# Weight loads of a three-part transformer kernel moved within the queue that issues them

## Chip, cores and metric

The kernel runs on one core of a Trainium2 chip, in one launch. The metric is device time: 3499.77 us, the median of three runs (3498.44 to 3503.96).

## The reference

The input is 4 sequences of 512 tokens with 128 features, in float32. Four stages follow one another, each added to its input and each applied to the layer-normalised activations: a chunked linear attention, a transformer of 6 layers, a retention layer with decay, and the same 6-layer transformer again, with the same weights. The transformers take nearly all the time. One layer of them is, in the reference's terms:

```python
def shift_tokens(t):            # second half of the features comes from the token before
    a, s = jnp.split(t, 2, -1)
    s = jnp.pad(s, ((0, 0), (1, 0), (0, 0)))[:, :-1]
    return jnp.concatenate([a, s], -1)
def attn_layer(x, Wqkv, qs, ksc, Wo):     # 16 heads of 64
    q, k, v = jnp.split(x @ Wqkv, 3, -1)
    ...
    q = l2norm(q) * qs
    k = l2norm(k) * ksc
    # rotary turn with a scale that grows by position, in q, and its inverse in k
    out = local_attention(q, k, v)        # windows of 32 queries on 64 keys, softmax
    return out @ Wo
def ffn_layer(x, g, bln, W1, b1, W2, b2): # 128 -> 2 x 341 -> 128
    xn = (x - mu) / jnp.sqrt(var + 1e-05) * g + bln
    a, gate = jnp.split(xn @ W1 + b1, 2, -1)
    return a * jax.nn.gelu(gate, approximate=False) @ W2 + b2
for i in range(DEPTH):
    x = attn_layer(shift_tokens(x), ...) + x
    x = ffn_layer(shift_tokens(x), ...) + x
```

## The kernel before

Activations stay on chip, transposed (features on partitions), in `xT` and `zT`. `stage_a`, `stage_ffn(0)`, `stage_b`, `stage_ffn(1)` and `finish` run in that order. The change is in `stage_ffn`, which is used twice; we call the two uses phase 0 and phase 1.

**Steps.** `stage_ffn` goes through 24 pairs of layer and sequence (6 layers, 4 sequences each) and makes one step of each pair. A step is a software pipeline of two halves: `cur` is the attention of the sequence at hand, `prev` is the rest of the sequence before it: its last values, output projection, and the whole second part of the layer (gates, hidden values, second product). So 25 steps run, 0 to 24; step 0 has no `prev`, step 24 no `cur`. The first step of a new layer is step 4, 8, ...; its `prev` half still belongs to the old layer. The output weights `wout` and the second-stage weights `w1`, `w2`, `pf` of a new layer are therefore needed one step later than its projection weights.

**Quads.** The 16 heads are worked in 4 quads of 4 heads. For each quad PE projects queries and keys (L626 to L628; the weights are split in two parts, `wh` and `wl`, and the product made in three matmuls), ACT squares the result (L809) and scales it into `ab` (L810), POOL adds the squares (L923), PE sums them over the head (`norms`, L645), ACT makes the inverse norms (L821, L823), DVE and POOL turn and scale (L964 to L978, L927 to L932). Then SP copies keys and queries to the layout that the score matmuls want, PE makes the scores (`scores`, L663), DVE subtracts the maximum (L984, L987), ACT takes exponentials (L827), DVE normalises and transposes (L993 to L1002), SP copies the transposed probabilities to `tb`, and PE multiplies them with the values (`values`, L684). ACT's `evacuate(g)` for quad g waits for the key and query copies of quad g - 2 (L805, L806), since they read the half of `ab` that it overwrites. PE's `values(g)` waits for the copies of the probabilities (`t_dma`, L675).

**The order on each engine is written out by hand.** Every engine has a function `step(s, prev, cur)` that lists its work in order, and they meet in semaphores that count up over the whole run; `now.count(signal, at)` gives the value to wait for. An engine takes its instructions in order, so whatever stands behind a waiting one waits as well.

**SP is the queue of the transfers.** All transfers within the loop are issued by SP. Its helpers in `step` are: `keys(g)`, 8 transfers of 64 KB (L516), after a wait for the turned keys; `queries(g)`, 4 of 128 KB (L526); `weights(g)`, 8 of the probabilities (L534 to L539), after a wait for the transpose `p_tr`; `next_tokens()`, 2 (L546, L547). The name weights(g) is for attention weights, that is probabilities, not for parameters; an index of -1 means quad 3 of the sequence before. The order within a step is keys(0), queries(0), next_tokens, weights(-1), keys(1), queries(1), weights(0), keys(2), queries(2), weights(1), keys(3), queries(3), weights(2).

**Parameters.** `load_qkv(rows, quads)` issues three transfers for a quad (384 KB, 384 KB and 2 KB; L479, L480), `load_out` one of 512 KB (L483), `load_ff` four (341, 128, 42.5 and 4.5 KB; L486 to L489). In the last step of a layer (3, 7, ..., 19) the projection weights of the next layer are loaded: quad 0 ahead of keys(2), quad 1 behind queries(2), quads 2 and 3 at the end, behind weights(2). In the first step of the new layer (4, 8, ..., 20) `wout` is loaded behind queries(2) and `load_ff` stands at the end, behind weights(2) and a wait for `x2`, the last addition of the sequence before, which no longer needs the old weights. PE waits for `w_ff` ahead of the gate matmuls (L779).

**SP's loops.** Step 0 stands alone. Then comes an outer loop over the layer changes (L589) whose body has an inner loop over two ordinary steps (L584), the step that loads the next layer, and the first step of the new layer. Behind the loop an inner loop over three ordinary steps and step 24 follow. The body holds the code of three steps for four that run. The other engines have one plain loop over steps 1 to 23.

`SP_USES` lists the multipliers and offsets of the counts that SP waits for, so that they can be computed once a step.

Of the kernel before, what the change touches and what calls it, by code (L numbers as in the profile page):

```python
# [3 lines left out]
def build_hybrid(nc, x_in, tabs, wa, wb, wf, out):  # L4
# [13 lines left out]
    B, N = 4, 512  # L18
    TOK = B * N
    DEPTH, HEADS, DH, WIN = 6, 16, 64, 32  # L20
# [10 lines left out]
    with ctx:  # L31
# [331 lines left out]
        STEPS = DEPTH * B  # L363
# [30 lines left out]
        x2 = Signal("x2", 1, 1, 4)  # L394
# [3 lines left out]
        w_out, w_ff = Signal("w_out", 16), Signal("w_ff", 64)  # L398
        GRANTED = [xs_done, x_hi, x_lo, n_ready, rope_q, rope_k, k_dma, q_dma, s_ready, s_sub, p_tr, t_dma, *o_ready, *o_read, x2, val_done]

        SP_USES = [(1, -1), (1, 0), (1, 1), (1, 3), *((4, c) for c in range(-2, 2)), (8, -4), (8, 0)]
        PE_USES = [(1, -1), (1, 0), (1, 2), (2, -2), (3, -5), (3, -4), (3, -3), (3, 0), *((4, c) for c in range(-4, 1)),
                    *((8, c) for c in (-12, -8, -7, -6, -5, -4, -3, -2, -1, 0)), *((16, c) for c in range(-15, 1)),
                    *((256, c) for c in range(-128, 65, 64)), *((512, c) for c in range(-640, 129, 128))]
# [7 lines left out]
        def stage_ffn(phase):  # L412
            scope = ExitStack()
            with scope:
# [33 lines left out]
                L0, FIRST = phase * DEPTH, phase * STEPS  # L448
# [17 lines left out]
                def _(sp):  # L466
# [15 lines left out]
                    def load_out(at):  # L482
                        sp.dma_start(wout[:, :, :], wf["wout"][bass.ds(at, 1)].rearrange("l (k p) n -> p (l k) n", p=128)).then_inc(w_out.sem, 16)  # L483

                    def load_ff(at):
                        sp.dma_start(w1[:, :], wf["w1"][bass.ds(at, 1)].rearrange("l c n -> (l c) n")).then_inc(w_ff.sem, 16)  # L486
                        sp.dma_start(w2[:, 0:2, :], wf["w2"][bass.ds(at, 1), 0:256].rearrange("l (k p) n -> p (l k) n", p=128)).then_inc(w_ff.sem, 16)
                        sp.dma_start(w2[0:FFC[2], 2, :], wf["w2"][bass.ds(at, 1), 256:FF].rearrange("l p n -> (l p) n")).then_inc(w_ff.sem, 16)
                        sp.dma_start(pf[:, :], wf["pf"][bass.ds(at, 1)].rearrange("l c n -> (l c) n")).then_inc(w_ff.sem, 16)  # L489
# [7 lines left out]
                        sp.dma_start(dst, src).then_inc(consts, 16)  # L497
                    load_qkv(rows_of_layer(0), range(1, QUADS))
                    load_out(0)
                    load_ff(0)  # L500

                    def step(s, prev, cur, new_layer=None, next_layer=None):
                        now = Steps(sp, s + 1, SP_USES)

                        if next_layer is not None:
# [22 lines left out]
                        def weights(g):  # L528

                            sp.wait_ge(o_ready[1].sem, now.count(o_ready[1], g - 1))  # L530
                            sp.wait_ge(p_tr.sem, now.count(p_tr, g))
                            for r in range(4):
                                rows = slice(32 * r, 32 * r + 32)
                                sp.dma_start(tb[rows, r], ptb[rows, 1]).then_inc(t_dma.sem, 16)  # L534

                                if r:
                                    sp.dma_start(tb[32 * r - 32:32 * r, r], ptb[rows, 0]).then_inc(t_dma.sem, 16)
                                else:
                                    sp.dma_start(tb[96:128, 4, 0:12], ptb[rows, 0, 4:16]).then_inc(t_dma.sem, 16)  # L539
# [12 lines left out]
                            next_tokens()  # L552
                        if prev:
                            weights(-1)
                        if cur:
                            keys(1)
                            queries(1)
                            weights(0)
                            if next_layer is not None:


                                sp.wait_ge(v_ready.sem, now.count(v_ready, TILES - 1))
                                load_qkv(layer_rows, range(1))
                            keys(2)
                            queries(2)
                            if next_layer is not None:
                                load_qkv(layer_rows, range(1, 2))
                            if new_layer is not None:
                                sp.wait_ge(wo_ready.sem, now.count(wo_ready, -1))
                                load_out(new_layer)  # L570
                            weights(1)
                            keys(3)
                            queries(3)
                            weights(2)
                            if next_layer is not None:

                                sp.wait_ge(v_ready.sem, now.count(v_ready, 2 * TILES - 1))
                                load_qkv(layer_rows, range(2, QUADS))
                            if new_layer is not None:
                                sp.wait_ge(x2.sem, now.count(x2, -1))  # L580
                                load_ff(new_layer)

                    def later_sequences(first, end):
                        with sp.Fori(1, end) as b:  # L584
                            step(first + b, True, True)

                    sp.wait_ge(zeroed, 2)
                    step(FIRST, False, True)
                    with sp.Fori(1, DEPTH) as at:  # L589
                        later_sequences(FIRST - B + at * B, B - 1)  # L590
                        step(FIRST - 1 + at * B, True, True, next_layer=at)
                        step(FIRST + at * B, True, True, new_layer=at)
                    later_sequences(FIRST + STEPS - B, B)
                    step(FIRST + STEPS, True, False)

                @block.tensor
# [738 lines left out]
```

## Time and profile before

| | |
|---|---|
| median of three runs | 3499.77 us |
| lowest, highest | 3498.44, 3503.96 us |
| the profiled execution | 3499.11 us |
| span of its trace | 3497.3 us |
| PE busy | 3165.8 us, 91% |
| DVE busy | 2895.0 us, 83% |
| ACT busy | 2273.7 us, 65% |
| POOL busy | 1808.8 us, 52% |
| mean granted TensorE clock | 0.951 |
| issues of f_kb, f_tb | 1536 of 64 KB, 1344 of 64 KB; 2.0 us to landing |
| issues of f_qb | 768 of 128 KB; 2.4 us to landing |
| issues of f_wh, f_wl | 48 each of 384 KB; 3.3 and 3.5 us to landing |

The busy times are sums over the whole span. PE is the busiest, but its share says nothing of when it stands still; that is read from the rows of single instructions. SP has no busy time in this table, since issuing a transfer isn't counted; its issues stand in the timeline as rows of SPq, with the time that each took to issue. "To landing" is the time from the issue to the arrival of the last byte. In the part of phase 0 between 541 and 1566 us lie steps 5 to 20, in the part of phase 1 between 2200 and 3260 us most of steps 4 to 20.

### The profile page before, as it was taken

What the parts mean: (1) busy time and instruction counts of PE and PEld (TensorE: products, weight loads), DVE (VectorE), ACT (ScalarE), POOL (GpSimd) and SP (SyncE); (2) the same over time, 40 slices, a digit from 0 to 9 for tenths busy, and PEclk for the clock granted to TensorE, in tenths of its full rate; (3) what the DMA queues carried; (4) which work ended last, traced back from release to release, by engine and by line L of the source; (5) the groups of instructions that cost most, each with busy time, mean ns of one, the idle gap of its engine ahead of it and who ended that gap; (6) DMA issues with size and microseconds to landing.
All of it is one profiled execution on the core that took longest, in us unless ns stands there. A gap on an engine that the chain in (4) does not pass through costs nothing. (4 is left out here: it accounts for less than half of the span.)

```text
span 3497.3 us, 71552 instructions
## 1 busy us (share of the span) xinstructions
PE 3165.8 (91%) x25368; PEld 1997.4 (57%) x25560; DVE 2895.0 (83%) x2723; ACT 2273.7 (65%) x3693; POOL 1808.8 (52%) x823
## 2 busy tenths in 40 slices
PE   5769999999999999999956899999999999999996
PEld 3536655655656666666533566666666566566563
DVE  4559988988988988988924899898898898898994
ACT  1147776766766776777712677677777777777773
POOL 5535555555555555555500555555565555555551
PEclk8789999999999999999977999999999999999998
DMA  5444454454454554554411445445445445445442
GB/s 183 160 116 101 111 135 107 116 127 109 115 130 107 122 124 104 122 127 108 99 34 66 101 104 140 114 97 144 109 103 141 110 105 140 105 111 137 111 111 60
DMA packets 273778, 399.12 MB, mean 114 GB/s; under 512 B 75836, under 2 KB 104248, under 8 KB 273720
## 3 DMA queue, kind: packets, MB, share of 16 engines
q1 hardware_dynamic: 273720, 398.48, 46.4%
q8 instruction: 20, 0.33, 0.0%
q14 instruction: 38, 0.31, 0.0%
HBM read 66.34 MB, written 19.92 MB: 25 GB/s over the span
## 5 line engine op out<-in xcount | busy, mean ns | idle before, releaser
L927 POOL TENSOR_TENSOR f_w<-f_w,f_ab 128x1024 f32<-128x1024 f32 x192 | 554.9, 2890 | 568.2 <-DVE f_w L964 568.2
L923 POOL TENSOR_TENSOR f_u<-f_u 128x512 f32<-128x512 f32 x384 | 582.0, 1530 | 464.0 <-ACT f_u L809 464.0
L932 POOL TENSOR_TENSOR f_ab<-f_w,f_rn 128x1024 f32<-128x1024 f32 x192 | 588.3, 3064 | 321.8 <-DVE f_rn L974 310.7
L809 ACT ACTIVATE f_u<-ps 128x512 f32<-128x512 f32 x768 | 466.6, 608 | 162.9 <-PE ps L628 84.9
L810 ACT ACTIVATE f_ab<-ps,f_pa 128x512 f32<-128x512 f32 x768 | 540.8, 704 | 1.2
L964 DVE TENSOR_TENSOR f_w<-f_ab,f_tan 128x1024 f32<-128x1024 f32 x384 | 498.9, 1340 | 4.6 <-POOL f_ab L932 4.6
L626 PE MATMUL ps<-f_xh,f_wh 128*128 128x512 f32 x768 | 384.2, 500 | 118.3 <-ACT f_ab L810 100.6
L684 PE MATMUL ps<-f_tb,f_v 128*64 128x160 f32 (+1 forms) x6144 | 446.9, 299 | 18.4 <-DMA f_tb<-f_pt 17.1
L684 PEld LDWEIGHTS ps<-f_tb,f_v 128*64 128x64 f32 x6144 | 400.2, 139 | 107.7 <-issue 105.0
L663 PEld LDWEIGHTS ps<-f_kb,f_qb 128*32 128x32 f32 x12288 | 351.2, 117 | 161.4 <-issue 128.3
L821 ACT ACTIVATE ps<-ps 128x512 f32<-128x512 f32 x384 | 204.6, 574 | 359.2 <-PE ps L645 359.2
L663 PE MATMUL ps<-f_kb,f_qb 128*32 128x128 f32 x12288 | 409.5, 290 | 24.5 <-DMA f_qb<-f_ab 24.5
L645 PE MATMUL ps<-f_u,f_ones 128*128 128x512 f32 x768 | 371.0, 605 | 9.1 <-DVE f_ones L1074 6.5
L699 PE MATMUL ps<-f_ot,f_wout 128*128 128x512 f32 x768 | 366.5, 600 | 1.7 <-DVE zT L1062 1.7
L984 DVE TENSOR_REDUCE f_mx<-ps 128x16 f32<-128x1024 f32 x192 | 233.3, 1215 | 140.1 <-PE ps L663 139.2
L827 ACT ACTIVATE f_p<-f_p 128x1024 f32<-128x1024 f32 x192 | 203.2, 1058 | 198.6 <-DVE f_p L987 198.6
L993 DVE TENSOR_REDUCE f_rs<-f_p 128x16 f32<-128x1024 f32 x192 | 233.4, 1216 | 116.5 <-ACT f_p L827 116.5
L978 DVE TENSOR_TENSOR f_ab<-f_w,f_rn 128x1024 f32<-128x1024 f32 x192 | 310.6, 1618 | 6.6
L628 PE MATMUL ps<-f_xh,f_wl 128*128 128x512 f32 x768 | 308.8, 402 | 0.0
L627 PE MATMUL ps<-f_xl,f_wh 128*128 128x512 f32 x768 | 307.7, 401 | 0.0
L999 DVE TENSOR_TENSOR f_p<-f_p,f_rs 128x1024 f32<-128x1024 f32 x192 | 280.6, 1462 | 1.8
L626 PEld LDWEIGHTS ps<-f_xh,f_wh 128*128 128x128 f32 x768 | 147.6, 192 | 233.4 <-ACT f_ab L810 138.4
(169 smaller groups left out, 5034.2 us busy)
## 6 DMA issues: line engine op xcount, KB each, us to landing
f_kb<-f_ab SPq DMA_DIRECT2D x1536, 64.0 KB, 2.0
f_qb<-f_ab SPq DMA_DIRECT2D x768, 128.0 KB, 2.4
f_tb<-f_pt SPq DMA_DIRECT2D x1344, 64.0 KB, 2.0
f_wh<-split_w SPq DMA_DIRECT2D x48, 384.0 KB, 3.3
f_wl<-split_w SPq DMA_DIRECT2D x48, 384.0 KB, 3.5
a_w_raw<-wqkv SPq DMA_DIRECT2D x24, 384.0 KB, 4.0
split_w<-a_w_hi SPq DMA_DIRECT2D x24, 384.0 KB, 2.3
split_w<-a_w_lo SPq DMA_DIRECT2D x24, 384.0 KB, 2.8
```

Source lines behind the costliest of these rows:

```text
L626: nc.tensor.matmul(bank("qk", g, i), wh[:, g, i, :], xh[:, :], start=True, stop=False)
L645: last = nc.tensor.matmul(ps[:, NO[i], :], ones[:, :], u[:, 2 * i + 1, :], start=True, stop=True)
L663: last = nc.tensor.matmul(ps[rows, SS[tile // 2], c0:c0 + 128], qb[:, pair, w0:w0 + WIN], kb[:, pair, :, w0:w0 + 2 * WIN], start=False, st ...
L684: last = nc.tensor.matmul(ps[rows, NO[pair], 128 * tile:128 * tile + WIN * windows], v[:, tile, d0:d0 + 64], tb[:, 0:windows, tile * HQ + ...
L699: last = nc.tensor.matmul(f, wout[:, 2 * g + i, :], ot[:, 2 * g + i, :], start=g + i == 0, stop=g + i == QUADS)
L809: nc.scalar.activation(u[:, i, :], bank("qk", g, i), ACT.Square).then_inc(sq_done.sem, 1)
L810: nc.scalar.activation(ab[:, g % 2, i, :], bank("qk", g, i), ACT.Identity, scale=pa[:, g, i:i + 1]).then_inc(qk_read.sem, 1)
L923: nc.gpsimd.tensor_tensor(u[:, 2 * i + 1, :], u[:, 2 * i, :], u[:, 2 * i + 1, :], ALU.add).then_inc(sq_sum[i].sem, 1)
L927: nc.gpsimd.tensor_tensor(w[:, 0:2, :], w[:, 0:2, :], ab[:, k % 2, 0:2, :], ALU.add).then_inc(q_sum.sem, 1)
L932: nc.gpsimd.tensor_tensor(ab[:, k % 2, 0:2, :], w[:, 0:2, :], rn[:, 0:1, :].broadcast_to([128, 2, N]), ALU.mult).then_inc(rope_q.sem, 1)
L964: nc.vector.tensor_tensor(w[:, a:4:2, :], ab[:, k % 2, 1 - a:4:2, :], tan2[:, a:a + 1, :].broadcast_to([128, 2, N]), ALU.mult).then_inc(tu ...
L978: nc.vector.tensor_tensor(ab[:, k % 2, 2:4, :], w[:, 2:4, :], rn[:, 1:2, :].broadcast_to([128, 2, N]), ALU.mult).then_inc(rope_k.sem, 1)
```

## The change

`load_ff` is taken out of the start of a phase and out of the end of a new layer's first step. In its place it stands in the step after that (steps 1, 5, 9, ..., 21), behind weights(-1) and ahead of keys(1), behind a wait for `x2` of two sequences back. The loads of quads 2 and 3 in the last step of a layer, with their wait for the last value projection, move from behind weights(2) to ahead of it. The inner loops are written out as steps, so that the one with `hidden_layer` can differ: the body of the outer loop then holds the code of four steps. `SP_USES` gets the offset that the new wait needs.

```diff
-        SP_USES = [(1, -1), (1, 0), (1, 1), (1, 3), *((4, c) for c in range(-2, 2)), (8, -4), (8, 0)]
+        SP_USES = [*((1, c) for c in range(-1, 3)), *((4, c) for c in range(-2, 2)), (8, -4), (8, 0)]
...
                     load_out(0)
-                    load_ff(0)
-
-                    def step(s, prev, cur, new_layer=None, next_layer=None):
+
+                    def step(s, prev, cur, hidden_layer=None, next_layer=None, new_layer=None):
...
                         if prev:
                             weights(-1)
+                        if hidden_layer is not None:
+
+                            sp.wait_ge(x2.sem, now.count(x2, -2))
+                            load_ff(hidden_layer)
                         if cur:
                             keys(1)
...
                             keys(3)
                             queries(3)
-                            weights(2)
                             if next_layer is not None:
 
                                 sp.wait_ge(v_ready.sem, now.count(v_ready, 2 * TILES - 1))
                                 load_qkv(layer_rows, range(2, QUADS))
-                            if new_layer is not None:
-                                sp.wait_ge(x2.sem, now.count(x2, -1))
-                                load_ff(new_layer)
-
-                    def later_sequences(first, end):
-                        with sp.Fori(1, end) as b:
-                            step(first + b, True, True)
+                            weights(2)
 
                     sp.wait_ge(zeroed, 2)
                     step(FIRST, False, True)
                     with sp.Fori(1, DEPTH) as at:
-                        later_sequences(FIRST - B + at * B, B - 1)
+                        step(FIRST - 3 + at * B, True, True, hidden_layer=at - 1)
+                        step(FIRST - 2 + at * B, True, True)
                         step(FIRST - 1 + at * B, True, True, next_layer=at)
                         step(FIRST + at * B, True, True, new_layer=at)
-                    later_sequences(FIRST + STEPS - B, B)
+                    step(FIRST + STEPS - 3, True, True, hidden_layer=DEPTH - 1)
+                    with sp.Fori(1, 3) as b:
+                        step(FIRST + STEPS - 3 + b, True, True)
                     step(FIRST + STEPS, True, False)
```

## Rows read from the trace of the kernel before

**Rows 1.** The page, part 1: busy us (share) x instructions of each engine.

```profile
PE 3165.8 (91%) x25368; PEld 1997.4 (57%) x25560; DVE 2895.0 (83%) x2723; ACT 2273.7 (65%) x3693; POOL 1808.8 (52%) x823
```

**Rows 2.** Timeline of DVE: start, us, line; steps 1, 3, 4, 5, 23; 1, 23.

```profile
326.94 0.68 DVE L1055 TENSOR_TENSOR f_xl<-f_xs,f_xh 128x512 fp32r<-128x512 f32 x1
...
450.20 0.68 DVE L1055 TENSOR_TENSOR f_xl<-f_xs,f_xh 128x512 fp32r<-128x512 f32 x1
...
515.80 0.68 DVE L1055 TENSOR_TENSOR f_xl<-f_xs,f_xh 128x512 fp32r<-128x512 f32 x1
...
584.06 0.68 DVE L1055 TENSOR_TENSOR f_xl<-f_xs,f_xh 128x512 fp32r<-128x512 f32 x1
...
1735.24 0.68 DVE L1055 TENSOR_TENSOR f_xl<-f_xs,f_xh 128x512 fp32r<-128x512 f32 x1
...
2031.40 0.68 DVE L1055 TENSOR_TENSOR f_xl<-f_xs,f_xh 128x512 fp32r<-128x512 f32 x1
...
3428.28 0.68 DVE L1055 TENSOR_TENSOR f_xl<-f_xs,f_xh 128x512 fp32r<-128x512 f32 x1
```

**Rows 3.** Timeline of ACT, first square of quad 2; steps 3, 4, 5, 21; [idle before].

```profile
417.95 0.59 ACT L809 ACTIVATE f_u<-ps 128x512 f32<-128x512 f32 x1
...
482.14 0.60 ACT L809 ACTIVATE f_u<-ps 128x512 f32<-128x512 f32 x1 [2.48 <-DMA f_qb<-f_ab]
...
550.00 0.60 ACT L809 ACTIVATE f_u<-ps 128x512 f32<-128x512 f32 x1 [4.76 <-DMA f_qb<-f_ab]
...
1578.28 0.60 ACT L809 ACTIVATE f_u<-ps 128x512 f32<-128x512 f32 x1 [1.80 <-DMA f_qb<-f_ab]
```

**Rows 4.** Timeline of SP's issues around the starts of steps 3, 4, 5; phase 1's 5.

```profile
408.17 4.96 SPq L516 DMA_DIRECT2D f_kb<-f_ab  x8
...
464.47 0.54 SPq L534 DMA_DIRECT2D f_tb<-f_pt  x1
...
472.78 4.95 SPq L516 DMA_DIRECT2D f_kb<-f_ab  x8
...
534.48 0.59 SPq L537 DMA_DIRECT2D f_tb<-f_pt  x1
...
536.94 0.36 SPq L489 DMA_DIRECT2D f_pf<-pf  x1
540.65 4.95 SPq L516 DMA_DIRECT2D f_kb<-f_ab  x8
...
2242.68 0.35 SPq L489 DMA_DIRECT2D f_pf<-pf  x1
2243.90 4.95 SPq L516 DMA_DIRECT2D f_kb<-f_ab  x8
```

**Rows 5.** Source line L589; DMA queues from 541 to 1566 us: packets, MB, share.

```profile
L589 SPq COMPARE_BRANCH  x10: 40/45/45, 537.4 to 3261.9; - x10
...
q14 instruction: 18, 0.15, 0.0%
```

**Rows 6.** PE in timeline and windows (PE busy, clock, DMA share, GB/s).

```profile
410.29 2.29 PE L684 MATMUL ps<-f_tb,f_v 128*64 128x160 f32 x32
...
484.00:487.00 3.00, 3.00 (x50) 0.50 0.46 109
...
1579.51 0.79 PE L626 MATMUL ps<-f_xh,f_wh 128*128 128x512 f32 x1 [2.67 <-ACT f_ab L810]
...
2000.47 0.50 PE L626 MATMUL ps<-f_xh,f_wh 128*128 128x512 f32 x1 [1.56 <-ACT f_ab L810]
```

**Rows 7.** Page, part 6, keys; then L516 from 477 to 477.7 us.

```profile
f_kb<-f_ab SPq DMA_DIRECT2D x1536, 64.0 KB, 2.0
...
DMA to landing us min/median/max: 2.6/2.8/3.0
```

**Rows 8.** Timeline of step 2: SP's keys(1) and PE's scores(1).

```profile
361.27 4.99 SPq L516 DMA_DIRECT2D f_kb<-f_ab  x8
...
372.07 1.95 PE L663 MATMUL ps<-f_kb,f_qb 128*32 128x128 f32 x64
```

## Prediction

> Steps are numbered within a phase as in the code: step 0 to step 24, each with the second half of the sequence before it. Steps 3, 7, 11, 15, 19 load the next layer's projection weights ("next steps"), steps 4, 8, 12, 16, 20 are the first of a new layer ("new steps"), steps 5, 9, 13, 17, 21 follow them ("hidden steps"). Quads are 0 to 3.
>
> **What bounds the kernel now.** I read the page's table of busy time first: PE 91%, no other engine above 83% [rows 1]. The chain of waits that ended last gives nothing here: it breaks off at once at the last addition on DVE. So I took one DVE instruction that runs once a step (L1055) from the timeline and took its distances [rows 2]. Steps 1 to 3 are 123.26 us apart over two intervals, 61.63 each. The interval that ends in new step 4 is 65.60, the one that ends in hidden step 5 is 68.26. From step 1 to step 23 there are 22 intervals, 1408.30 us in phase 0 and 1396.88 in phase 1; at 61.6 each they would be 1355.2. So 53.1 + 41.7 = 94.8 us is all that layer changes cost, 10 new and 10 hidden steps, and no edit of the weight loads can win more.
>
> Where it is lost shows in ACT's rows at the first square of quad 2 (L809) [rows 3]. In step 3 it starts at 417.95 with no idle time. In step 4 ACT idles 2.48 us before it, in step 5 4.76, in step 21 1.80, each time for the query transfers of quad 0 (`queries(0)`). PE then stands still, since its banks aren't read out, and comes back at a granted clock of 0.50, that is 1.2 instead of 2.4 GHz [rows 6]: that is the remainder of the excess (65.60 - 61.6 - 2.48 = 1.5 us in step 4). So a boundary costs its ACT stall plus some 1.5 us of low clock; step 21, with 1.80, some 3.3.
>
> And the queries are late because SP, which issues every transfer at about 0.62 us each, is late with `keys(0)` [rows 4]. In step 3 keys(0) starts at 408.17; a step later it would be due at 469.8 and starts at 472.78, because the loads of quads 2 and 3 stand between weights(2) and it: weights(2) starts at 464.47, eight issues take it to 469.45, the loads take 3.3 us. Before step 5 weights(2) ends at 534.48 + 0.59 = 535.07, `load_ff` at 537.30, and then SP issues nothing until 540.65: 5.58 us from weights(2) to keys(0). In phase 1 the same place shows 2243.03 to 2243.90, a gap of 0.87 rather than 3.35.
>
> That gap is code. Here the outer loop of SP branches back (L589, ten times); between 541 and 1566 us, phase 0, the DMA view has 18 packets of instructions, and none between 2200 and 3260, phase 1 [rows 5]. The bodies are the same; so phase 0's just doesn't stay in the engine's instruction store, and phase 1's just does.
>
> **The change, part by part.**
>
> *(a) Loads of quads 2 and 3 ahead of weights(2), 10 places.* SP's time is conserved: from the start of keys(3) to keys(0) it runs without a pause (queries(3) ends at 464.37, weights(2) starts at 464.47), the v_ready wait has long been met, so weights(2) starts 3.1 us later and keys(0) of the new step still starts at 472.8. The stall of quad 2 isn't removed. What is new: the last of the eight transfers is issued at 472.0 instead of 468.86. Behind such loads a 64 KB transfer at the same distance took 2.8 us to land instead of the 2.0 of an undisturbed one [rows 7]: 474.8 to 475.0. PE's `values(-2)` (L684), which needs them, starts at 410.29 in step 3, so is due at 471.9 in step 4 [rows 6]. PE waits 2.9 us there. Behind it stand the rest of project_v(0), norms(1), and by them ACT's inverse_norms(1) and quad 2: ACT is ready for quad 2 at 479.66 + 2.9 = 482.6, the queries are there at 482.14. The two delays lie beside each other, and +0.5 us is left. The clock: PE idle for 2.67 us came back with its matmul at 0.79 us, PE idle for 1.56 us at 0.50 [rows 6], so 2.9 us costs the same 1.5 us as now, only earlier; the second pause is then under 1 us. Value: 10 x 0.5 = +5. Ends: -1.0 a place if the clock isn't lowered (0.5 - 1.5), +2.0 if it is lowered twice (0.5 + 1.5); I take the middle because 2.9 is nearer to the row of 2.67 than to that of 1.56.
>
> *(b) load_ff out of the turn from the new to the hidden step.* Phase 0, four turns over the outer branch (steps 5, 9, 13, 17): the 2.2 us of load_ff go, the 3.35 of the branch stay, keys(0) and queries(0) come 2.2 us earlier, the ACT stall falls from 4.76 to 2.6. That is still a pause like step 4's, so the low clock stays: -2.2 x 4 = -8.8. Ends: 0 and, if stall and clock both went, -6.6 a place.
>
> Phase 1, four turns: the body now writes out four steps instead of looping over one of three (each about 82 transfers and some 15 other instructions), so it is over a quarter longer. What overflowed in phase 0 at the shorter length should now overflow in both. The gap grows from 0.87 to 3.35 while 2.2 us go: +0.3 x 4 = +1.2. Ends: +0.3 a place, and -3.7 if the code still stays.
>
> The Trainium skill ("Runtime: NRT & Kernel Launch", Instruction fetch mechanics) says that an engine holds two blocks of 256 instructions and that a taken branch out of these stops for a fetch. The trace agrees with the stop and shows its price, 3.35 us less some 0.5 of register work. By that rule a body of about 436 instructions would stay if it started in the first 76 of a block, three times in ten. It is the rule that would bring rival 2 below.
>
> Last turn of each phase (into step 21): no branch back, neither before nor after. load_ff goes, keys(0) follows weights(2) as from step 2 to 3, and stall and clock go: -3.3 x 2.
>
> *(c) load_ff between weights(-1) and keys(1) of steps 1, 5, ..., 21.* It adds four issues and a wait for x2 of two steps back, done long before (its writer L1062 runs half a step earlier): 2.2 us. Queued behind it are keys(1), queries(1), weights(0). In an undisturbed step keys(1) starts at 361.27 and PE's scores(1) (L663) at 372.07 [rows 8]. Eight issues of keys and four of queries put the last at 368.2; with the 2.4 us that the page's table of transfers gives for f_qb it lands at 370.6. So the slack is 1.5 us, 0.7 us come through to PE, and half of that is lost again in ACT's own queue, which is the longer one there: +0.4 in steps 1 and 21 (4 in all: +1.6). In steps 5 to 17 keys(1) waits for scores(0) anyway (the low clock draws these scores out, and SP is there first), so it is hidden. Ends: 0 and +0.7. w1 and w2 are needed some 25 us later by PE's gate matmuls; hidden. The loads taken out of the start of each phase stood ahead of a wait of 5 us and more for the first keys: nothing. The inner loop's branch (0.7 us) lay in slack: nothing.
>
> **Sum.** +5.0 - 8.8 + 1.2 - 6.6 + 1.6 = -7.6 us. The profiled execution took 3499.11 (span 3497.3 and 1.8 around it) and the median is 3499.77; from the latter the forecast is 3492 us. The measurement tells about 0.2%, 7 us, from nothing, so this lies on the edge of what can be told.
>
> **Rivals.**
> 1. PE's pause at values(-2) doesn't lower the clock (two pauses of 2.9 and under 1 us instead of one of 3.35). For it: 1.56 us didn't. Against: 2.67 did. It saves 1.5 in each of 10 places: 3492 - 15 = 3477.
> 2. The longer body stays in the store in phase 1. For it: the body fits there now, and the page's rule. Against: the same body doesn't fit in phase 0. Then each of four turns is 0.9 us from weights(2) to keys(0) instead of 3.1, stall and clock go, -3.7 instead of +0.3: 3492 - 16 = 3476.
> 3. Slower: weights(2) behind 1.5 MB of loads. The eight transfers of probabilities queue behind the loads, values(-2) waits over 4 us, and PE comes back slow, so that ACT's quad 2 is later than the queries by more than the parts (b) give: these are worth 12.6 us, so the point is 1.3 us a place over ten places. For it: transfers right behind the loads are visibly slower [rows 7] and the slack at values(-2) is only about 1 us (last issue some 0.95 ahead of 408.17, landing at 409.2, use at 410.29). Against: five microseconds of issuing lie between the last load and the last of them. At +2.5 a place: 3499.8 + 25 - 12.6 = 3512; at +2.0, 3507.
> 4. The change moves things only: (a) costs 1 us a place, or fetches fall on other places, and all cancels: 3497 to 3503.
>
> **Chances.** Forecast 50% (3485 to 3498, 27 of the 50 below 3492.8, the rest within 0.2%), rival 1 14%, rival 2 10%, rival 3 15%, rival 4 11%. Faster by over 0.2%: 27 + 14 + 10 = 51%; within: 23 + 11 = 34%; slower: 15%. The range takes in both faster rivals but their tails and rival 3 up to +2.0: 3474 to 3507.
>
> **What would show it.** In the new steps keys(0) still about 3 us late and ACT's stall before quad 2 gone or small, with a PE wait before L684 for the probabilities of 2 to 3 us in its place; if that wait isn't there, (a) is wrong. In hidden steps of both phases a gap of some 3.3 us on SP before keys(0), with instruction packets in phase 1 too, and an ACT stall of 2.6; no gap in phase 1 is rival 2. Into step 21 an interval of 62. L1055's distances give the sum directly: per layer 66.1 and 66.1 in phase 0, 66.1 and 65.7 in phase 1.

## The result: 0.9926 of the time before

The changed kernel took 3475.39 us (median of 4 runs, 3471.86 to 3479.21), the kernel before beside it 3499.82 (3498.44 to 3503.96). The ratio is 0.9926, with a 95% interval of 0.9914 to 0.9938: 24.4 us faster, where 7.6 were forecast. The time lies at the fast edge of the range, where rivals 1 and 2 stood.

The profiled execution took 3471.86 us (span 3470.1, mean granted clock 0.958). First the page's busy times, beside [rows 1]: PE is busy 20 us less with the same number of matmuls. The work is the same; some of it ran at the higher clock.

```profile
PE 3145.8 (91%) x25368; PEld 1982.1 (57%) x25560; DVE 2906.5 (84%) x2723; ACT 2275.1 (66%) x3693; POOL 1816.8 (52%) x823
```

DVE's instruction that runs once a step (L1054 now), timeline; steps 1, 3, 4, 5, 23 of phase 0, then 1 and 23 of phase 1, as in [rows 2]:

```profile
332.94 0.68 DVE L1054 TENSOR_TENSOR f_xl<-f_xs,f_xh 128x512 fp32r<-128x512 f32 x1
...
456.20 0.68 DVE L1054 TENSOR_TENSOR f_xl<-f_xs,f_xh 128x512 fp32r<-128x512 f32 x1
...
520.57 0.68 DVE L1054 TENSOR_TENSOR f_xl<-f_xs,f_xh 128x512 fp32r<-128x512 f32 x1
...
586.06 0.68 DVE L1054 TENSOR_TENSOR f_xl<-f_xs,f_xh 128x512 fp32r<-128x512 f32 x1
...
1721.44 0.68 DVE L1054 TENSOR_TENSOR f_xl<-f_xs,f_xh 128x512 fp32r<-128x512 f32 x1
...
2016.64 0.68 DVE L1054 TENSOR_TENSOR f_xl<-f_xs,f_xh 128x512 fp32r<-128x512 f32 x1
...
3403.84 0.68 DVE L1054 TENSOR_TENSOR f_xl<-f_xs,f_xh 128x512 fp32r<-128x512 f32 x1
```

New step 4 is 64.37 us (65.60 before), hidden step 5 65.49 (68.26 before). The 22 intervals of a phase make 1388.50 and 1387.20 us; over the 1355.2 of undisturbed steps that is 33.3 + 32.0 = 65.3, where it was 94.8.

ACT's first square of quad 2 in steps 3, 4, 5 and 21, as in [rows 3]; in brackets the idle time before it:

```profile
423.96 0.60 ACT L808 ACTIVATE f_u<-ps 128x512 f32<-128x512 f32 x1
...
488.41 0.60 ACT L808 ACTIVATE f_u<-ps 128x512 f32<-128x512 f32 x1 [0.33 <-DMA f_qb<-f_ab]
...
552.41 0.60 ACT L808 ACTIVATE f_u<-ps 128x512 f32<-128x512 f32 x1 [2.38 <-DMA f_qb<-f_ab]
...
1565.97 0.60 ACT L808 ACTIVATE f_u<-ps 128x512 f32<-128x512 f32 x1
```

The stall of step 4 is 0.33 us (2.48), that of step 5 2.38 (4.76), that of step 21 gone (1.80). Then SP's issues, as in [rows 4]; the last two lines are phase 1's hidden step 5:

```profile
414.06 4.94 SPq L515 DMA_DIRECT2D f_kb<-f_ab  x8
...
473.86 0.56 SPq L533 DMA_DIRECT2D f_tb<-f_pt  x1
...
479.05 4.95 SPq L515 DMA_DIRECT2D f_kb<-f_ab  x8
...
539.47 0.58 SPq L536 DMA_DIRECT2D f_tb<-f_pt  x1
543.05 4.95 SPq L515 DMA_DIRECT2D f_kb<-f_ab  x8
...
2224.84 0.59 SPq L536 DMA_DIRECT2D f_tb<-f_pt  x1
2228.48 4.95 SPq L515 DMA_DIRECT2D f_kb<-f_ab  x8
```

In step 4 keys(0) starts 3.39 us later than a step of 61.6 after step 3's: SP is still as late as before (3.01 then), even 0.4 us later. In hidden steps the gap from weights(2) to keys(0) is 3.00 us in phase 0 (5.58 before) and 3.05 in phase 1 (3.09 before, most of it load_ff then). The DMA queues from 541 to 1566 us (phase 0) and from 2200 to 3260 (phase 1), packets, MB, share, beside [rows 5]:

```profile
q14 instruction: 24, 0.20, 0.1%
```

```profile
q14 instruction: 21, 0.17, 0.0%
```

Phase 1 had no packet of instructions before. It has 21 now.

**The budget.** ACT's squares of quad 3 give each step's length. Summed over 61.6, in us, for two traces of each kernel (the second pair is from the runs after_again and before_again below):

```
                        forecast   before        after         measured change
10 new steps            +5.0       44.8, 44.4    35.4, 41.4     -6.2
hidden 5..17, phase 0   -8.8       27.1, 27.0    15.4, 14.2    -12.3
hidden 5..17, phase 1   +1.2       16.3, 16.2    14.4, 14.3     -1.9
two steps 21            -6.6 +0.8   6.4,  6.7     0.1,  0.1     -6.4
two steps 1             +0.8        1.4,  1.7     3.9,  3.4     +2.1
sum                     -7.6                                   -24.7
```

So the forecast missed in the first three lines: by 11.2 us in the new steps, where even the sign was wrong, and by 3.5 and 3.1 in the turns. The steps of the table make 24.7 us, but the traces' spans differ by 21.0 in the mean (3497.3 and 3495.3 before, 3470.1 and 3480.6 after). Nearly all of the rest is the time before phase 0's first L1055, at 205.60 and 210.51 us before and at 211.12 and 212.18 after; over all traces of this study it lies between 205.6 and 213.6, and nothing here explains it.

### The profile page after: what moved, and what is told of

Read it like the earlier page. It is cut to its first block and busy times, and to the rows that moved or that the text cites. A ratio compares the mean times of both kernels' runs of the same rounds, so it can differ in the third digit from the quotient of the medians.

```text
span 3470.1 us, 71421 instructions
## 1 busy us (share of the span) xinstructions
PE 3145.8 (91%) x25368; PEld 1982.1 (57%) x25560; DVE 2906.5 (84%) x2723; ACT 2275.1 (66%) x3693; POOL 1816.8 (52%) x823
## 5 line engine op out<-in xcount | busy, mean ns | idle before, releaser
L922 POOL TENSOR_TENSOR f_u<-f_u 128x512 f32<-128x512 f32 x384 | 589.4, 1549 | 452.6 <-ACT f_u L808 451.9
L683 PE MATMUL ps<-f_tb,f_v 128*64 128x160 f32 (+1 forms) x6144 | 452.6, 301 | 44.9 <-DMA f_tb<-f_pt 43.6
L683 PEld LDWEIGHTS ps<-f_tb,f_v 128*64 128x64 f32 x6144 | 404.4, 140 | 135.6 <-issue 99.9
L662 PEld LDWEIGHTS ps<-f_kb,f_qb 128*32 128x32 f32 x12288 | 338.0, 113 | 158.7 <-issue 119.0
L662 PE MATMUL ps<-f_kb,f_qb 128*32 128x128 f32 x12288 | 392.9, 282 | 28.0 <-DMA f_qb<-f_ab 27.9
L714 PE MATMUL ps<-f_fq,f_w 128*128 128x512 f32 (+1 forms) x576 | 271.2, 609 | 7.6 <-issue 5.9
```

The lines of the kernel that those rows point to most:

```text
L662: last = nc.tensor.matmul(ps[rows, SS[tile // 2], c0:c0 + 128], qb[:, pair, w0:w0 + WIN], kb[:, pair, :, w0:w0 + 2 * WIN], start=False, st ...
L683: last = nc.tensor.matmul(ps[rows, NO[pair], 128 * tile:128 * tile + WIN * windows], v[:, tile, d0:d0 + 64], tb[:, 0:windows, tile * HQ + ...
L922: nc.gpsimd.tensor_tensor(u[:, 2 * i + 1, :], u[:, 2 * i, :], u[:, 2 * i + 1, :], ALU.add).then_inc(sq_sum[i].sem, 1)
```

## The experiments

The theory that they test: PE's pause ahead of values(-2), which the moved loads bring, is about 2.8 us long, and at this length the lower clock follows only in some places, while the forecast took it for all. Rivals are that the new body, or part (b), brought the gain, and that the loads themselves (1.5 MB in flight) and not the pause decide about the clock. Ratios are to the kernel before on the same chip, with 95% intervals; "new" and "hidden" are the sums over ten such steps, as in the budget (before: 44.8 and 49.8). Where a step is said to have the lower clock, the trace grants 0.50 for a stretch behind its pause.

**Part (a) alone.** The kernel before with the block moved up:

```diff
+    if next_layer is not None:
+        sp.wait_ge(v_ready.sem, now.count(v_ready, 2 * TILES - 1))
+        load_qkv(layer_rows, range(2, QUADS))
     weights(2)
-    if next_layer is not None:
-        sp.wait_ge(...); load_qkv(...)
```

> The kernel before with part (a) alone: the loads of quads 2 and 3 ahead of weights(2). Theory: keys(0) of the new step stays as late as it was, PE now pauses 2.4 to 3.1 us before values(-2) instead of 3.4 us before quad 2, and in most of the 10 places that pause doesn't lower the clock. New steps then cost 2.8 us over an ordinary one where the clock stays and 4.7 where it falls, against 4.0 to 5.3 before; about -10 us in all, 3490 us. Rival: (a) gives nothing by itself, the gain is all of load_ff's move: 3500 us, new steps at 4.0 to 5.3 over. My own prediction had 3505.

3494.71 against 3500.20 us, 0.9982 (0.9972 to 0.9992). New 37.2, hidden 46.0. The new steps gain 7.6 where the forecast had them lose 5; in four of the ten places they are 2.5 to 2.9 us over, in the others 3.8 to 5.0. In phase 1 three hidden steps (2.26, 2.28 and 1.79 over) lack the lower clock too. The two steps 1 were 5.7 over (before 1.4), without part (c); with these 4.3 us the whole came to 3495 instead of the 3490 expected.

**Parts (b) and (c) alone.** The changed kernel with weights(2) back ahead of the loads:

```diff
+    weights(2)
     if next_layer is not None:
         sp.wait_ge(...); load_qkv(layer_rows, range(2, QUADS))
-    weights(2)
```

> The changed kernel with the loads of quads 2 and 3 put back behind weights(2): load_ff's move and the written-out body alone. Theory: hidden steps 3.5 to 3.9 us over an ordinary one in both phases, step 21 none, new steps as before (4.0 to 5.3), the first steps of a phase some 1.2 us slower each: 3499.8 - 20 + 2.4 = 3482 to 3485 us. Rival, that (a) gives nothing: 3475 us.

3489.04 us, 0.9966 (0.9954 to 0.9979). Hidden 29.3, which is after's 29.8, and new 48.8. So (a) gains in the new steps (7.6) and (b) in the hidden ones (20.5), as the budget has it for both together. By the medians the parts make 5.5 + 11.2 = 16.7 of 24.4 us. What lacks is in the steps 1 (7.3 over here, 1.4 before) and in this kernel's new steps, 4.0 above before: ACT's stalls in front of quad 2 are 2.3 us longer there in sum (28.2 against 25.8), and in six of the ten places, not four, the lower clock lasted longer and cost 2.3 us and more (below). Why the stalls and the steps 1 are longer is open.

**The longer body alone.** The kernel before with its inner loop written out and the loads of w1 and w2 at their old places:

```diff
     with sp.Fori(1, DEPTH) as at:
-        later_sequences(FIRST - B + at * B, B - 1)
+        step(FIRST - 3 + at * B, True, True)
+        step(FIRST - 2 + at * B, True, True)
```

> The kernel before with the body of the outer loop written out as four steps, nothing moved. If SP's pause at the branch back is code that no longer stays in its store: instruction packets in phase 1 too, the gap before keys(0) of steps 5, 9, 13, 17 in phase 1 grows from 0.87 to 3.3 us, with load_ff still ahead of it, so these four steps go from 3.7 to some 6.5 us over an ordinary one: +11 us, 3511 us. Rival: the longer body stays, or the gap has another cause (registers, the x2 wait): 3500 us and no packets.

3518.41 us, 1.0055 (1.0038 to 1.0071), slower. Hidden steps of phase 1: 30.6 instead of 19.5, +11.1. The timeline of SP in phase 1's step 5 shows the last issue before the branch and keys(0):

```profile
2251.44 0.36 SPq L489 DMA_DIRECT2D f_pf<-pf  x1
2255.05 4.97 SPq L516 DMA_DIRECT2D f_kb<-f_ab  x8
```

3.25 us without an issue, where [rows 4] has 0.87; and from 2200 to 3260 us 24 packets of instructions:

```profile
q14 instruction: 24, 0.20, 0.1%
```

So it is the written-out body that brings the stop at the branch into phase 1, by itself, and the rest of part (b) that pays for it. The gain isn't the body's. Phase 0's hidden steps lost 3.7 us as well, 1.7 of it in step 21; that part, and the 7 us by which the time lies over the expected 3511, were not followed up.

**The same loads, one turn earlier.** The changed kernel with the block between weights(1) and keys(3), where SP has slack:

```diff
     weights(1)
+    if next_layer is not None:
+        sp.wait_ge(...); load_qkv(layer_rows, range(2, QUADS))
     keys(3)
     queries(3)
-    if next_layer is not None:
-        sp.wait_ge(...); load_qkv(layer_rows, range(2, QUADS))
     weights(2)
```

> The changed kernel with the loads of quads 2 and 3 between weights(1) and keys(3), where SP idles 3.5 us for the turned keys. Theory: the loads (3.3 us of issuing) fit there, keys(0) of the new step is on time, neither PE nor ACT pauses, new steps cost 0 to 0.5 us over an ordinary one instead of 2.8 to 4.7: -33 us, 3442 us. Rival 1: keys(3) or its landing gets late by the 1.5 MB in front of it, and 1 us a place comes back: 3452. Rival 2: what a new step costs isn't SP's lateness but its new weights: 3475, as it is.

3441.28 us, 0.9839 (0.9821 to 0.9857). The DVE instruction of steps 3, 4 and 5:

```profile
454.67 0.68 DVE L1054 TENSOR_TENSOR f_xl<-f_xs,f_xh 128x512 fp32r<-128x512 f32 x1
...
516.27 0.68 DVE L1054 TENSOR_TENSOR f_xl<-f_xs,f_xh 128x512 fp32r<-128x512 f32 x1
...
580.63 0.68 DVE L1054 TENSOR_TENSOR f_xl<-f_xs,f_xh 128x512 fp32r<-128x512 f32 x1
```

New step 4 takes 61.60 us. New 0.0, hidden 28.9: the whole of a new step's excess comes of the 3.2 us of issuing between two transfers that are waited for.

The hidden steps, where only the branch is left, show the clock once more. PE's first matmul behind its pause, in step 5 of phase 0 and of phase 1:

```profile
549.14 0.50 PE L625 MATMUL ps<-f_xh,f_wh 128*128 128x512 f32 x1 [3.09 <-ACT f_ab L809]
...
2211.16 0.80 PE L625 MATMUL ps<-f_xh,f_wh 128*128 128x512 f32 x1 [3.13 <-ACT f_ab L809]
```

Behind the first the clock stayed up and the step is 2.8 us over, behind the second it fell and the step is 4.8 over. All four turns of phase 0 kept the clock, with pauses of 3.07 to 3.25 us, and all four of phase 1 lost it, with 3.09 to 3.14.

**The loads split.** The changed kernel with quad 2's loads ahead of weights(2) and quad 3's behind:

```diff
-    load_qkv(layer_rows, range(2, QUADS))
+    load_qkv(layer_rows, range(2, 3))
     weights(2)
+    if next_layer is not None:
+        load_qkv(layer_rows, range(3, QUADS))
```

> The changed kernel with the load of quad 2 ahead of weights(2) and that of quad 3 behind it. SP's time to keys(0) is the same. Theory: what a new step costs is SP's lateness of 2.5 to 2.8 us; the low clock comes on top only where one single pause of PE is long. Here the pause is cut in two, some 1.2 us at values(-2) and some 2 us ahead of quad 2, so the clock stays in all 10 places: new steps at 2.5 to 2.8 over an ordinary one, 26 us instead of 35 in sum, 3466 us. Rival: the sum of the pauses decides, or chance: new steps still at 4 or more in several places, 3475 us.

3470.25 against 3502.68 us, 0.9918 (0.9901 to 0.9934). New 36.7: five phase 0 steps with 5.61, 5.62, 4.15, 4.33 and 2.87, and phase 1's five with 2.78 to 2.84. PE's pause is now ahead of quad 2; its timeline after such a pause, step 4 of phase 0 and of phase 1:

```profile
485.81 0.79 PE L627 MATMUL ps<-f_xh,f_wh 128*128 128x512 f32 x1 [2.80 <-ACT f_ab L811]
...
2172.63 0.50 PE L627 MATMUL ps<-f_xh,f_wh 128*128 128x512 f32 x1 [2.78 <-ACT f_ab L811]
```

Two pauses of one length, 2.80 and 2.78 us, and the first matmul behind them takes 0.79 us once and 0.50 the other time. Four of phase 0's five places had the lower clock, none of phase 1's. I had expected the new steps at 26 and two short pauses; the one at values(-2) was 0.8 to 0.9 us and left the other at 2.8. Without the lower clock a place costs 2.8 us, near the 2.5 to 2.8 expected; that the clock would stay up was wrong.

**No loops on SP.** The changed kernel with its steps written out one by one, so that nothing branches and all addresses and counts are constants:

```diff
-    with sp.Fori(1, DEPTH) as at:
-        step(FIRST - 3 + at * B, True, True, hidden_layer=at - 1)
-        ...
+    for n in range(1, STEPS):
+        step(FIRST + n, True, True, hidden_layer=..., next_layer=..., new_layer=...)
```

> The changed kernel with SP's 25 steps written out without a loop, nothing moved. Theory: the hidden steps' cost (3.5 to 3.9 us each in 8 places) is the fetch of code behind SP's branch back; straight code is fetched ahead. No gap before keys(0) of steps 5, 9, 13, 17, no ACT stall there: -28 us, 3447 us; new steps as they are. Rival: the fetches of straight code, one each 128 instructions, stop SP as well, spread over all steps: ordinary steps over 61.6 us and 3475 us or more.

3454.90 against 3502.68 us, 0.9862 (0.9845 to 0.9878). Steps 3, 4 and 5 on DVE:

```profile
457.04 0.68 DVE L1049 TENSOR_TENSOR f_xl<-f_xs,f_xh 128x512 fp32r<-128x512 f32 x1
...
523.45 0.68 DVE L1049 TENSOR_TENSOR f_xl<-f_xs,f_xh 128x512 fp32r<-128x512 f32 x1
...
585.06 0.68 DVE L1049 TENSOR_TENSOR f_xl<-f_xs,f_xh 128x512 fp32r<-128x512 f32 x1
```

Hidden step 5 takes 61.61 us, and all ten together are 0.2 over: with load_ff moved, what is left of a hidden step is the branch with its register work. Straight code fetched as well (12 packets of instructions from 541 to 1566 us) and stopped nothing. The new steps cost 51.3 here, more than before the change: the eighth transfer of probabilities landed 2.9 to 3.7 us after its issue (2.0 to 2.8 in the changed kernel), the pauses were 2.86 to 3.69 us, and nine of ten had the lower clock. So the kernel came to 3455 instead of the 3447 expected.

**Both.** The kernel without loops and with the loads one turn earlier, that is, on top of the edit of flat:

```diff
     weights(1)
+    if next_layer is not None:
+        load_qkv(layer_rows, range(2, QUADS))
     keys(3)
     queries(3)
```

> Both: no loop on SP, and the loads of quads 2 and 3 between weights(1) and keys(3). Theory: every step of both phases at 61.6 us but the first ones: 3441 - 28 = 3413 us. Rival: straight code stops SP for fetches: 3441 or more.

3407.73 us, 0.9733 (0.9717 to 0.9749), 5 us under the expected 3413. And the same with layer 0's w1 and w2 loaded at the start of each phase again, so that step 1 has no such loads:

```diff
     load_out(0)
+    load_ff(0)
...
-    hidden_layer=n // B if n % B == 1 else None
+    hidden_layer=n // B if n % B == 1 and n > 1 else None
```

> flat_early with the first layer's load_ff back at the start of each phase, so that step 1 has none ahead of keys(1). Theory: load_ff cost the two steps 1 1.2 us each in the changed kernel where its addresses came from registers; with constants, as here and in step 21, it costs about nothing: 0 to -2.4 us against flat_early, 3411 to 3413 us. Rival: at the start it delays the first keys: +3 us a phase, 3419.

3404.36 us, 0.9723 (0.9707 to 0.9740), the fastest version of this study, 71 us below the changed kernel. Steps 1 and 23 of each phase on DVE:

```profile
329.85 0.68 DVE L1050 TENSOR_TENSOR f_xl<-f_xs,f_xh 128x512 fp32r<-128x512 f32 x1
...
1685.39 0.68 DVE L1050 TENSOR_TENSOR f_xl<-f_xs,f_xh 128x512 fp32r<-128x512 f32 x1
...
1978.48 0.68 DVE L1050 TENSOR_TENSOR f_xl<-f_xs,f_xh 128x512 fp32r<-128x512 f32 x1
...
3334.12 0.68 DVE L1050 TENSOR_TENSOR f_xl<-f_xs,f_xh 128x512 fp32r<-128x512 f32 x1
```

22 intervals in 1355.54 and 1355.64 us: 61.6 each. The 94.8 us that the prediction gave as all that layer changes cost are all gone. The 3.4 us between the last two versions are too few to be told from nothing; the two steps 1 cost 1.2 us here and 2.4 in flat_early.

**The two kernels once more,** unchanged, for how much of it is drawn anew in each execution:

> The changed kernel once more, for its spread and a second trace. The stalls are set by the order and should repeat to 0.1 us (SP's gap of 2.8 to 3.0 us before keys(0) of the hidden steps; PE's pause of 2.4 to 3.2 us before values(-2) of the new steps). If the low clock after such a pause is a draw, the number of new steps with it (3 of 10 in the first trace) changes, and the total with it by 1.9 us each; if it follows from the pause's length, the same three have it. Time 3472 to 3479.

> The kernel before once more, for a second trace: the low clock behind each of its 20 pauses (2.7 to 5.6 us) again, new and hidden steps 94 us over ordinary ones in sum; the time up to the first step of phase 0, 209.7 us in the first trace and 212 to 218 in all others, tells whether that part moves by itself. 3496 to 3506 us.

after_again took 3479.54 against 3502.09 us, 0.9931 (0.9915 to 0.9947); before_again 3497.14 in its one run. The kernel before repeats itself (new 44.4, hidden 49.9). The changed kernel's new steps came out at 41.4 instead of 35.4: six of ten had the lower clock, two of them where it was the first time, when it was four (the expectation says three, which was a miscount). Nor did the pauses repeat to 0.1 us as expected: that of step 4 in phase 0 was 2.38 us in the first trace and 4.14 in the second, because the eighth transfer of probabilities landed 3.8 us after its issue and not 2.0. That is the width of the theory's own term. The part ahead of phase 0 moves by itself: 4.9 us longer in before_again than in the first trace of the same kernel.

**The kernel before without loops,** its loads at their old places:

```diff
-    with sp.Fori(1, DEPTH) as at:
-        later_sequences(FIRST - B + at * B, B - 1)
-        ...
-    later_sequences(FIRST + STEPS - B, B)
+    for n in range(1, STEPS):
+        step(FIRST + n, True, True, new_layer=..., next_layer=...)
```

> The kernel before with SP's steps written out without a loop, load_ff and the loads where they were. Theory: the fetch behind the branch back is gone, load_ff's 2.2 us ahead of keys(0) stay: all ten hidden steps cost what steps 21 did, 3.2 to 3.3 us, 33 us in sum instead of 50; new steps as before: -17 us, 3483 us. Rival: the branch costs by its registers, not by the fetch, and phase 1 gains as much as phase 0: 3475 us.

3469.99 against 3502.09 us, 0.9906 (0.9891 to 0.9920). New 42.7, hidden 21.4. I had expected 33 in the hidden steps. With constants SP is through from weights(2) to keys(0) in 2.03 us instead of 2.63, so ACT's stall is 1.2 us instead of 1.8; and in steps 17 and 21 of both phases the clock stayed up behind the same pause (1.2 us over instead of 2.7 to 2.8). Turning SP's loops into straight code is alone worth 32 us, more than the change under study.

**A ladder of delays.** The fastest version, with 6 to 11 idle transfers of 2 KB between queries(3) and weights(2) of the next steps, so that weights(2) is late with no large loads in flight:

```diff
+    for _ in range(((6, 7, 8, 9, 10), (10, 9, 8, 7, 11))[phase][next_layer - 1]):
+        sp.dma_start(spare[:, next(spare_loads)], wf["pa"][0]).then_inc(spared, 16)
     weights(2)
```

> flat_early_ff0, whose new steps cost nothing, with idle transfers of 2 KB (into a tile that nobody reads) in front of weights(2) in steps 3, 7, 11, 15, 19: 6, 7, 8, 9, 10 of them in phase 0 and 10, 9, 8, 7, 11 in phase 1, at 0.47 us of issuing each. So PE's pause before values(-2) is set: about 1.8 us with 6 (2.8 late less 1.0 of slack), 0.47 more with each, 4.2 with 11. Theory now, after two traces of the changed kernel: a new step costs its pause, and 1.5 to 2.6 us more where the pause is near 3 us or longer; so 6 to 8 transfers cost 1.8 to 2.8 us and 9 to 11 cost 4.7 to 6.5. Rival: the low clock is a draw that doesn't follow the pause: both kinds among the short and the long ones. Second rival: it takes the 1.5 MB of loads, and no step here has the low clock. Sum over ten new steps about 30 + 5 x 2 = 40 us: 3445 us.

3459.06 against 3501.43 us, one run each, where 3445 was expected. New, 51.2 in sum: 2.53, 3.79, 4.58, 6.19, 6.38 with 6 to 10 transfers in phase 0; 5.59, 5.97, 5.81, 4.19, 6.14 with 10, 9, 8, 7, 11 in phase 1. PE's values(-2) in new steps 4, 8 and 20, timeline:

```profile
477.81 2.29 PE L684 MATMUL ps<-f_tb,f_v 128*64 128x160 f32 x32 [1.97 <-DMA f_tb<-f_pt]
...
727.40 3.62 PE L684 MATMUL ps<-f_tb,f_v 128*64 128x160 f32 x32 [2.48 <-DMA f_tb<-f_pt]
...
1483.07 4.32 PE L684 MATMUL ps<-f_tb,f_v 128*64 128x160 f32 x32 [4.12 <-DMA f_tb<-f_pt]
```

A pause is enough, without the large loads: from 470 to 475 us, ahead of step 4's pause, the DMA engines are busy for 0.28 here and for 0.98 in the changed kernel, and nine of ten places had the lower clock. The rival by which it takes the loads falls; flat_early_ff0 has the same loads one turn earlier, no pause and no lower clock in its new steps. But both places with 7 transfers (pauses of 2.48 and 2.68 us) and both with 8 (3.05 and 3.17) had the lower clock against my expectation, while pauses as long kept it in other kernels, so the length alone doesn't decide there either.

## Why the prediction was too small by a factor of three

**The step that failed** is the one on the clock in part (a): "PE idle for 2.67 us came back with its matmul at 0.79 us, PE idle for 1.56 us at 0.50 [rows 6], so 2.9 us costs the same 1.5 us as now, only earlier". It took one row at 2.67 us as what happens each time. The pause was sized well (2.38 to 3.17 us in the ten places, mean 2.82), and the price was wrong: the forecast had the new steps lose 5 us, and they gained 9.4 in one trace and 3.0 in the other. PE's values(-2) of the changed kernel in new steps 4, 12 and 16 of phase 0 (the second a part of its 32 matmuls) and step 4 of phase 1, in order of time:

```profile
480.33 2.29 PE L683 MATMUL ps<-f_tb,f_v 128*64 128x160 f32 x32 [2.38 <-DMA f_tb<-f_pt]
...
986.89 3.37 PE L683 MATMUL ps<-f_tb,f_v 128*64 128x160 f32 x28 [3.12 <-DMA f_tb<-f_pt]
...
1241.77 2.29 PE L683 MATMUL ps<-f_tb,f_v 128*64 128x160 f32 x32 [2.89 <-DMA f_tb<-f_pt]
...
2164.68 3.96 PE L683 MATMUL ps<-f_tb,f_v 128*64 128x160 f32 x32 [2.98 <-DMA f_tb<-f_pt]
```

And the four us behind the first and the second (window, busy sum, PE busy, granted clock, DMA share, GB/s):

```profile
480.00:484.00 4.00, 3.67 (x38) 1.00 0.42 98
...
987.00:991.00 4.00, 4.00 (x33) 0.57 0.42 99
```

The matmuls take 2.29 us at full clock, and 3.37 to 3.96 where 1.2 GHz was granted behind the pause. Four of ten places had it in the first trace, six in the second. In the two traces together the ten places without it cost 2.75 to 2.88 us, mean 2.80, and the ten with it 4.45 to 5.54, mean 4.88. The forecast comes to 4.98 a place (4.48 before and 0.5 more), which fits where the clock fell. So rival 1, with 14%, was what happened in half of the places; at 2.1 us a place over five of ten that is 10.4 us of the 11.2 missed in the new steps, and of the 17 in all.

The "1.5 us as now" was one row too. In the trace of the kernel before, four of the ten new steps are 5.2 to 5.4 us over and six 3.8 to 4.1, with much the same stalls (2.48 to 2.85 us): in the four the lower clock lasted twice as long, and cost 2.4 to 2.7 us instead of 1.2 to 1.5. The prediction read step 4 alone, which is one of the six.

The same term in the second trace, after_again, new steps 4 and 20 of phase 0:

```profile
484.23 3.57 PE L683 MATMUL ps<-f_tb,f_v 128*64 128x160 f32 x32 [4.14 <-DMA f_tb<-f_pt]
...
1502.21 2.29 PE L683 MATMUL ps<-f_tb,f_v 128*64 128x160 f32 x32 [2.39 <-DMA f_tb<-f_pt]
```

Point by point:

- **What bounds the kernel, and the ceiling of 94.8 us:** right. flat_early_ff0 shows that it can all be had.
- **(a) SP's time is conserved:** right but for 0.4 us. keys(0) of step 4 is 3.39 us late (forecast 3), ACT's leftover stall 0.33 (forecast 0.5), and the PE wait stands ahead of L683 as said. Where the clock stayed up the excess is these two alone: 2.38 + 0.33 of the 2.77 in step 4, 2.81 + 0 of the 2.79 in step 12 of phase 1.
- **(b) phase 0:** forecast -2.2 a place, measured -3.1. Both terms of it were a little small. The gap left at the branch is 2.74 to 3.04 us and not 3.35; a part of that is the registers of one loop less to set (0.13 us behind the branch instead of 0.36). And the lower clock cost about 1.5 us behind these pauses instead of 1.4 to 2.4, mean 2.0, behind the longer ones; "the low clock stays" held in seven of eight places of the two traces, that it costs the same did not.
- **(b) phase 1:** the mechanism is right, shown by unroll_only: the body overflows there as well, rival 2 is out. Forecast +0.3 a place, measured -0.5: the gap is 2.78 to 3.05 us and not 3.35, and the 2.7 us that the lower clock cost in one of the four places before is not there after. By the prediction's estimate from the Trainium skill ("Runtime: NRT & Kernel Launch", Instruction fetch mechanics) such a body would have stayed in the store three times in ten, by where it starts; of the two phases neither kept it, which decides nothing about three in ten. The body was sized a little large: the trace has 425 to 428 instructions of SP from one branch to the next, not 436. Of the ten branches of [rows 5] eight go back; the last of each phase doesn't.
- **(b) step 21:** right: 5.8 us net of (c) were forecast for both, and 6.4 measured.
- **(c):** forecast +0.4 in each step 1. The sum of both rose by 2.1, but in a_alone, without (c), it was 4.3 above before. Over all traces the two steps 1 cost 2.0 to 7.3 us with (c), mean 3.7 of seven, and 0.8 to 5.7 without, mean 1.9 of seven. So it is likely more than forecast, some 0.9 a place, but the spread leaves it open; no step 5 to 21 shows it.
- **Rival 3:** weights(2) behind the loads. Its mechanism is real: the eighth transfer landed 2.0 us after its issue in the kernel before, 2.0 to 2.8 in the changed one's first trace, 2.1 to 3.8 in its second and 2.9 to 3.7 in flat. PE's pauses follow it, in the mean 2.8, 3.1 and 3.3 us, up to 4.14 in after_again; in flat the new steps cost 51.3. In the changed kernel their sum stayed below that of the kernel before in both traces.

What stays open: which of two like pauses gets the lower clock, and for how long. The runs give counts and no rule.

## What to carry to other kernels

One row at a clock change is one case: before pricing ten places from it, look for as many rows of such pauses as the trace has, and give the price as a share of places. When a queue is late, don't only swap the order of what stands in the late stretch; look for the stretch in which the queue has slack (here one turn earlier, 34 us better than the change). And on an engine that only issues transfers, a loop whose body is long can cost a stop at every branch back. Writing it out was worth 32 us to the kernel before and 20 to the changed one, the best reordering 34 us (early), and both together 68. Writing out only a part of the loop (unroll_only) cost 18.

## What the hardware showed that I had not expected

- **Clock behind a pause of PE.** Ahead of values(-2), in the five traces with loads or idle transfers in front of weights(2) (after, after_again, a_alone, flat, ladder): of 29 pauses of 2.98 us and longer 28 were followed by 1.2 GHz, of 19 between 2.28 and 2.91 us 6 were, of the two at 1.97 and 2.09 none. Ahead of quad 2's first matmul the share is another: of 65 pauses of 3.3 us and longer all were, of 45 between 2.95 and 3.3 us 38, of 30 between 2.65 and 2.95 us 23, and of ten at 2.06 to 2.12 us (flat_before) 6. The same program had it in four of ten new steps in one execution and in six in another. These are the lengths of this kernel's pauses with its work around them, not a rule.
- **The first matmul doesn't tell.** In flat_before the pauses of steps 5 and 17 of phase 0 are both 2.08 us and the first matmul behind both takes 0.50 us; in step 5 the clock fell a moment later, which cost 1.6 us, in step 17 it stayed. The prediction took that duration as its sign; the granted clock of a window behind it says more.
- **A branch back that leaves the instruction store** costs SP 2.74 to 3.75 us between two transfers, 2.4 to 3.5 of it from the branch to the next instruction, where a body that stays costs 0.83 to 0.86 between them. Whether a body of about 340 instructions stays in differed between two copies of it: phase 0's never, phase 1's always, in both traces of the kernel before and in a_alone. At 425 to 428 instructions both were out, in all six traces.
- **Constants save little in the issues themselves.** The four issues of load_ff take 1.9 us with constants, 1.95 to 2.4 with addresses from registers, and in step 1 of the changed kernel's phase 0 once 2.6 and once 3.0. What writing out saved in flat_before is mostly the register work around them: 0.42 us from the last issue to keys(0) in step 21, and 0.10 with constants.
